# Layer 0 of a graph network: in odd halves VectorE mixes ahead of its two additions, in even halves behind them

## The reference

```python
edge_index = jnp.stack([src, dst])
xn = _layernorm(x, axis=-1)
x = x + gnn(xn, edge_index, ...) + mix(xn[None], ...)[0]
x = x + ffn(_layernorm(x, axis=-1)[None], ...)[0]

# gnn, twice:
neigh = x[col]
agg = jax.ops.segment_sum(neigh, row, num_segments=n)
h = (x + agg / deg) @ W.T + b            # then layernorm and silu

# mix, cut to its order (proj, expmap0 and logmap0 scale each row by a function of its norm):
h = relu(batchnorm(conv1d(logmap0(proj(x)), w_qkv)))     # 768 channels
s = conv1d(conv1d(t, w_dw), w_pw)                        # 768 more
q, k, v = jnp.split(qkv3, 3, axis=2)                     # 16 groups of 3 x 32
out = relu(q) * sum(v * relu(k)) / (v + eps)             # what the einsums come to for length 1
fx = proj(expmap0(conv1d(logmap0(proj(expmap0(out))), w_res) + b_res))
```

## Time and profile before

| what | us |
|---|---|
| median of 3 runs | 2906.38 |
| span of the profiled execution | 2910.9 |
| TensorE busy | 2211.4 (76%) |
| ScalarE busy | 1597.5 (55%) |
| GpSimd busy | 1526.8 (52%) |
| VectorE busy | 1510.5 (52%) |

### The profile page before, as it was taken

One profiled execution on the slowest core, in us unless ns is written; L12 is line 12 of the kernel. 1 busy time (PEld: TensorE's weight loads), 2 busy tenths in 40 slices (PEclk: granted clock), 3 DMA queues, 4 the chain that ended last, 5 costly groups with the idle time before them and its releaser, 6 DMA issues.

```text
span 2910.9 us, 35251 instructions
## 1 busy us (share of the span) xinstructions
PE 2211.4 (76%) x9037; PEld 1591.1 (55%) x9037; DVE 1510.5 (52%) x3581; ACT 1597.5 (55%) x3867; POOL 1526.8 (52%) x1591
## 2 busy tenths in 40 slices
PE   2377678787878787878767847778788888778699
PEld 1254356565656565656544535555555555556378
DVE  8899945555555555555513852344444444445611
ACT  5220077666666666666752655565655665565422
POOL 0000276555565556655773067777777777776000
PEclk9687688999999999999988778899999998899799
DMA  7110033333233233333335144444444444443322
GB/s 183 36 53 0 26 112 100 92 93 93 82 102 94 85 91 98 101 94 87 105 107 132 54 145 118 127 133 132 132 126 130 130 130 127 125 138 109 78 75 61
DMA packets 132041, 293.68 MB, mean 101 GB/s; under 512 B 31098, under 2 KB 76506, under 8 KB 128975
## 3 DMA queue, kind: packets, MB, share of 16 engines
q0 software_dynamic: 75584, 208.18, 24.6%
q1 hardware_dynamic: 17266, 44.84, 5.7%
q10 hardware_dynamic: 39000, 38.41, 4.4%
HBM read 259.31 MB, written 32.00 MB: 100 GB/s over the span
## 4 chain that ended last, share of the span: by engine, by line
PE 32%; POOL 26%; DVE 23%; issue 11%; ACT 5%; DMA 1%; DVEq 0%; ACTq 0%; SPq 0%; POOLq 0%
POOL whole L674 26%; PE ps L1234 9%; PE ps L1253 8%; DVE whole L1954 5%; DVE arena_a L1565 3%; PE ps L1483 3%; PE ps L1270 3%; DVE arena_a L1566 3%; PE ps L1322 2%; PE ps L1251 1%; DVE whole L1958 1%; ACT whole L816 1%; ACT whole L828 1%; ACT whole L823 1%; PE ps L1388 1%
## 5 line engine op out<-in xcount | busy, mean ns | idle before, releaser
L674 POOL DMA_INDIRECT whole<-table,arena_a x1568 | 1517.7, 968 | 912.5 <-issue 462.9
L1234 PE MATMUL ps<-whole 128*125 x3968 | 999.7, 404 | 260.1 <-SPq L572 99.4
L1234 PEld LDWEIGHTS ps<-whole 128*125 128x125 f32 x3968 | 773.2, 199 | 445.8 <-issue 322.7
L1900 DVE TENSOR_TENSOR whole<-ps,whole 125x257 f32 (+1 forms) x496 | 210.3, 424 | 1037.7 <-PE ps L1234 1012.4
L789 ACT ACTIVATE arena_b<-iota_row,arena_a 128x125 f32<-128x125 f32 (+1 forms) x1496 | 458.9, 387 | 80.2 <-PE ps L1234 37.1
L791 ACT ACTIVATE whole<-arena_b,ones 128x1000 f32<-128x1000 f32 (+1 forms) x248 | 279.9, 1128 | 8.1
L1253 PE MATMUL ps<-arena_b,whole 128*125 128x384 f32 x400 | 225.8, 704 | 0.0
L780 ACT ACTIVATE arena_b<-iota_row,arena_a 128x125 bf16<-128x125 f32 x488 | 153.5, 387 | 33.3 <-issue 23.0
L1251 PE MATMUL ps<-arena_b,ones 3*125 3x384 bf16 x100 | 46.4, 464 | 164.9 <-ACTq L829 164.9
L816 ACT ACTIVATE whole<-whole 125x512 f32<-125x512 f32 x50 | 31.6, 631 | 251.2 <-DVE whole L1958 251.2
L1954 DVE RECIPROCAL whole<-whole 125x512 f32<-125x512 f32 x50 | 167.7, 3353 | 1.7
(11 more groups left out here) (438 smaller groups left out, 3157.9 us busy)
## 6 DMA issues: line engine op xcount, KB each, us to landing
whole<-table,arena_a POOLq DMA_INDIRECT x1568
table<-whole SPq DMA_DIRECT2D x9, 1120.0 KB
whole<-table ACTq DMA_DIRECT2D x50, 125.0 KB
mix_rows<-whole ACTq DMA_DIRECT2D x50, 125.0 KB
arena_a<-table ACTq DMA_DIRECT2D x50, 125.0 KB
arena_b<-in_x_dram ACTq DMA_DIRECT2D x50, 125.0 KB
arena_b<-mix_rows ACTq DMA_DIRECT2D x50, 125.0 KB
x_rows<-whole ACTq DMA_DIRECT2D x50, 125.0 KB
```

What stands on the lines that cost most here:

```text
L674: pool.indirect_dma_start(gat[:, GRP * slot + k, 0:D], None, table[l], bass.IndirectOffsetOnAxis(ap=s_dst[:, n:n + 1], axis=0)).then_inc(s ...
L1234: mm = pe.matmul(ps[0:PT, banks[at % len(banks)], 0:width], onehot[:, ROUND * (r % 2) + QS * k + n, :], gat[:, bass.ds(slots[QS * k + n], ...
L1900: dve.tensor_tensor(to, ps[0:PT, banks[at % len(banks)], 0:width].unsqueeze(1), to, ALU.add).then_inc(s("agg_added"), 1)
```

## The change

In layer 0, VectorE's order is no longer the same in each half. In an odd half it does its mixing slot first and then the two additions; in an even half the additions come first, as before. TensorE's order and all others stay. No instruction and no wait is added or taken away.

```diff
+                def sums_and_slot(half):
+
+                    if half % 2 == 1 and half < SLOTS:
+                        mix_slot(half)
+                    if half < HALVES:
+                        additions(half)
+                    if half % 2 == 0 and half < SLOTS:
+                        mix_slot(half)
+
                 if l == 0:
-                    window(additions, mix_slot)
+                    for half in range(max(HALVES, SLOTS)):
+                        sums_and_slot(half)
```

## The result

The changed kernel takes 2702.94 us (median of 4 runs, 2701.50 to 2705.87), the kernel before beside it 2907.01. The ratio is 0.9296, 95% interval 0.9283 to 0.9309: 204 us less. The forecast was 2713, its range 2690 to 2765.

What follows compares the result with a forecast made beforehand. No engine was full; a ring of waits bounded layer 0's mixing, with GpSimd nearly the bound afterwards. 46 x (20.70 - 16.5) = 193 us saved, from a median of 2906.4 to 2713 us, range 2690 to 2765.

Steps and rivals of the forecast that it cites:

- The ring: Layer 0's mixing: TensorE, ScalarE, VectorE and GpSimd wait for each other; odd slot held back 5.7 us by two additions.
- Only part of the wait goes: Rival, chance 0.09: ScalarE's one-hots make the roots late, the slot starts half as much earlier; 80 us saved, 2826 us.
- Slower: Rival, chance 0.04: roots come after the odd products, the even slot comes 1.3 us later; 60 us more, 2966.
- The cover of the additions: Odd additions run about 2.5 us later on VectorE; products needing their banks come some 14 us later, so cost nothing.
- TensorE's own 15.5 us: TensorE's own work for one tile of the mixing at full clock, with the ring open: 15.5 us.
- The clock: TensorE's granted clock in the mixing stage should rise from 0.91 towards 1.00 without the gap of 3.50 us.
- GpSimd's floor: The mixing stage's 586 gathers with gaps of 0.30 take at least 747 us, 16.2 us a tile; saves 205 us.
- the allowance over the floor: Mixing stage: 16.5 us a tile taken in place of 16.2, for some remaining waits for a landing or a slot.
- The cross-check of the prediction: GpSimd's 47 waits for slots in the whole kernel, 222.5 us, less 47 x 0.30 still spent: cap of 208 us.
- the rival of gathers held up: Chance 0.06: VectorE's wide-row TENSOR_SCALARs, 1.3 us a tile, hold up GpSimd's gathers; 162 us saved, 2744 us.

Runs made afterwards that it cites:

- even_first: Against the kernel before: slot first in the even halves, additions first in the odd ones; ratio 0.9998, in the repeat 1.0117.
- between: Against the kernel before: in odd halves VectorE does one addition, then the slot, then the other addition; ratio 0.9874, in the repeat 0.9886.
- late_half: Odd halves below 56 as in the kernel before, those from 56 on as in the changed kernel; 2820.97 us, ratio 0.9705.
- pe_more: The changed kernel with four more short products with the bias row on TensorE in each tile; 2703.38 us, ratio 0.9298.

## Why the prediction was right

*The ring.* Right. The start of the odd slot was forecast 1.3 us ahead of the odd products (813.2 and 814.49), and it came 1.1 ahead (813.00 and 814.11). One detail differs: it isn't the roots that set it, which were there at 812.39 + 0.19, but the end of the even slot's line 1925. In the stage line 1930 waits 39 times for line 1925 and 7 times for line 841, at most 0.5 us, so the rivals in which the roots come late ("Only part of the wait goes" and "Slower") didn't happen. Line 1958 was forecast 5.1 us behind the start of the odd products and ended 5.25 behind it. The waits of lines 816 and 1251 went, but for one of 0.2 us each. That the odd additions close the ring, and the even ones don't, is shown by even_first (20.6) and between (17.3).

*The cover of the additions.* Right: 35 waits of line 1234 are put down to line 1900, which I had named as what would make the prediction wrong, but they last 0.38 us on average where "issue" stood with 0.34 before; one lasts 1.1 us. By the code the even products need the additions of two halves before, long done, not those at 819.73. It is the old gap under another name; what the one of 1.1 us was isn't known. Both slots first, with later additions, has 1.4 us of it.

*TensorE's own 15.5 us.* Right: 15.4 to 15.5 in most tiles, and fifteen in a row in late_half. The forecast went by the slower GpSimd, and the stage shows both: most tiles at 15.45, and a few of 20 to 23 us in which TensorE waits for landed rows.

*The clock.* Right in direction and size: 0.99 in the stage. Of the 11 waits for landed rows, four, of 2.7 to 4.4 us, have a lower clock behind them; the other seven, at most 1.6 us each, have 1.00. Between 725 and 728 us TensorE is nearly idle, and then it has 0.63:

```profile
725.00:728.00 3.00, 0.45 (x2) 0.42 (x3) 0.00 (x0) 2.65 (x10) 2.39 (x3) 1.00 0.51 149
728.00:731.00 3.00, 3.00 (x10) 1.80 (x9) 0.45 (x2) 1.27 (x2) 2.09 (x3) 0.63 0.36 105
```

*GpSimd's floor, and the 10 us of the miss.* The term mis-sized is the allowance over the floor: I took 16.5 us a tile against a floor of 16.2, and the stage took 16.12, so it gave 210.7 us where 193 were forecast. A tile can be below the floor since GpSimd starts the stage with rows stored ahead and ends it with fewer: 576 gathers fall into it where 586 did. What counts is the whole run of gathers. The first starts at 341.6 us and the last of layer 0 at 1348.97, where it was 342.4 and 1553.21:

```profile
1348.97 0.94 POOL L674 DMA_INDIRECT whole<-table,arena_a  x1 [0.30 <-issue]
```

That is 204.2 us earlier. The stage starts 4.3 us sooner and gives 210.7, and the gathers left behind it take 10.8 longer, since more of them are left. In the terms of GpSimd's 784 gathers: waits for slots fell from 222.5 to 2.1 us, the gaps of 0.30 grew by 13.3 us, the gathers themselves by 3.6, and the first starts 0.8 earlier. The cross-check of the prediction, 222.5 - 47 x 0.30 = 208, was the better estimate. The medians differ by the same 204 us. The two profiled spans differ by 209.9, and the 5.7 us beyond the last gather lie half ahead of layer 1 and half in it, where nothing was changed; the span of before was longer than every timed run of it, so I take them for scatter between executions. Of TensorE's waits for landed rows I had feared a cost; they cost nothing, because GpSimd doesn't stop for them: pe_more has 1.2 us of them in place of 20.0 and the same time.

*Gathers beside a denser VectorE.* 983 ns in place of 975, about 8 ns each, against the 0.10 us (46 x 1.3 / 586) that the rival of gathers held up would take. The rule of the Trainium skill that speaks against the change ("SBUF — State Buffer", section "SBUF: two separate sides") shows as little here as before: at 577 gathers it is some 5 us.

## What to carry to other kernels

When four engines wait for each other in turn and none is full, look for the first instruction on the ring whose own inputs are long there, and see what is queued ahead of it on its engine. If nobody waits for that, swap them. Then count each engine's own work per round: the largest is what the swap can reach, and a count of the waits that must vanish (here GpSimd's for slots) gives the saving more closely than an allowance by feel.

## What I had not expected of the hardware

A short piece of work put behind a gather costs GpSimd less than its own time: 116 ns of memset added 53 ns to a pair of gathers in the stage, 30 through a shorter gap behind it and the rest through gathers that show 18 ns less each, for a reason that these runs don't show. Four repeated matmuls of 384 columns with three rows cost 0.16 us each in a row, where the single one shows 0.37. And the clock added to the return of an earlier start: 1.6 us of it gave 3.3 us a tile, with 1.00 behind a gap of 1.79 us ahead of line 1251 where it was 0.91 over the stage with gaps of 3.50.
